# Where the mask of an attention is added: half of its score tiles move from TensorE to VectorE

## The reference

```
x = layernorm(x + L0(x, adj))   # attention of one head, 128 features
x = layernorm(x + L1(x, adj))   # attention of 8 heads of 32 features, the layer of this change
x = layernorm(x + L2(x, adj))   # sums over neighbours
x = layernorm(x + L3(x, adj))   # 4 heads of 256, then one more, then a feed-forward part
```

```
q, k, v = split_heads(h @ W.T + b)
scores  = einsum('bhqd,bhkd->bhqk', q, k) / sqrt(32)
scores  = where(adj == 0, -inf, scores)
attn    = softmax(scores);  out = (attn @ v) @ Wo.T + bo
```

## Time and profile before

| | |
|---|---|
| time, median of 3 runs | 3092.38 us (3091.72 to 3095.64) |
| the profiled execution | 3093.04 us, its span 3091.3 us |
| mean granted TensorE clock | 0.943 of full speed |
| L663, the mask on PE | 512 matmuls of 128 x 512, 134.1 us busy |
| L871, the exp of the scores | 512 instructions, 263.9 us busy |

### The profile page before, as it was taken

How to read it: one execution, slowest core, us unless ns; L and a number is a source line. 1 busy time by engine, 2 the same in 40 slices (tenths; PEclk the granted TensorE clock), 3 DMA queues, 4 the chain that set the end, 5 groups by cost and what they waited for, 6 DMA issues and landing times.

```text
span 3091.3 us, 47649 instructions
## 1 busy us (share of the span) xinstructions
PE 2725.8 (88%) x17668; PEld 2029.7 (66%) x17668; DVE 2070.4 (67%) x5503; ACT 1223.4 (40%) x2273; POOL 824.4 (27%) x640
## 2 busy tenths in 40 slices
PE   0679989899998989989898998989899998989976
PEld 0447776767767676766767677676767767676664
DVE  3547485775848677584867758486775858677563
ACT  0224435353443535344352543435254343524341
POOL 0113231322313232232323222232322323232231
PEclk9889989999898999989899998989999898999987
DMA  4000000000000000000000000000000000000000
GB/s 124 7 14 1 8 14 1 15 8 15 8 8 14 1 15 8 15 8 8 14 1 15 8 15 8 8 14 1 14 8 15 8 8 14 1 8 8 1 8 7
DMA packets 29763, 36.74 MB, mean 12 GB/s; under 512 B 2272, under 2 KB 23648, under 8 KB 29536
## 3 DMA queue, kind: packets, MB, share of 16 engines
q1 hardware_dynamic: 29536, 33.69, 3.7%
HBM read 25.30 MB, written 8.39 MB: 11 GB/s over the span
## 4 chain that ended last, share of the span: by engine, by line
PE 57%; DVE 23%; issue 8%; ACT 6%; POOL 4%; SPq 1%; DMA 1%; DVEq 0%; POOLq 0%; ACTq 0%
PE bank L587 12%; PE bank L546 9%; PE bank L784 7%; DVE bank L1077 5%; PE bank L673 4%; PE bank L561 4%; PE bank L679 4%; PE bank L540 4%; PE bank L663 3%; PE bank L656 3%; POOL exp_b L472 3%; DVE picked L1044 2%; PE bank L793 2%; DVE o_t L1121 2%; PE bank L713 2%
## 5 line engine op out<-in xcount | busy, mean ns | idle before, releaser
L472 POOL TENSOR_TENSOR exp_b<-exp_b,edge_t 128x512 int32<-128x512 int32 x320 | 455.0, 1437 | 1075.9 <-DVE exp_b L1065 1075.9
L587 PE MATMUL bank<-vals_b,exp_b 128*128 128x257 f32 x2560 | 662.6, 404 | 75.4 <-POOL exp_b L472 67.3
L587 PEld LDWEIGHTS bank<-vals_b,exp_b 128*128 128x128 f32 x2560 | 483.4, 198 | 231.8 <-POOL exp_b L472 117.7
L923 ACT ACTIVATE h_sb<-bank,rden_g_b 128x256 f32<-128x256 f32 x320 | 151.6, 474 | 692.5 <-DVE rden_g_b L1221 692.5
L1077 DVE CUSTOM_DVE_ANT_0 bank<-bank,edge_bias 128x512 f32<-128x512 f32 x512 | 338.9, 720 | 22.4 <-PE bank L605 21.5
L1065 DVE TENSOR_TENSOR exp_b<-exp_b,low_b 128x512 f32<-128x512 f32 x320 | 271.6, 870 | 93.1 <-ACT low_b L839 90.8
L1044 DVE CUSTOM_DVE_ANT_0 picked<-bank,edge_bias 128x512 bf16<-128x512 f32 x384 | 241.5, 683 | 108.9 <-PE bank L561 108.9
L871 ACT ACTIVATE exp_a<-bank 128x512 f32<-128x512 f32 x512 | 263.9, 608 | 89.4 <-PE bank L663 89.4
L818 ACT ACTIVATE vals_b<-bank 128x512 f32<-128x512 f32 (+1 forms) x192 | 100.9, 536 | 485.5 <-PE bank L784 280.7
L460 POOL TENSOR_TENSOR rstd_a<-var_eps_a,neg_half 128x4 f32<-128x4 f32 x48 | 51.2, 1067 | 777.5 <-DVE var_eps_a L1021 777.5
L784 PE MATMUL bank<-wo_sb,ht_all 128*128 128x259 f32 x1024 | 233.6, 383 | 0.8 <-ACT ht_all L818 0.8
(11 more groups left out here) (185 smaller groups left out, 5409.5 us busy)
## 6 DMA issues: line engine op xcount, KB each, us to landing
x_t<-in_x_t SPq DMA_DIRECT2D x16, 512.0 KB, 3.6
xa<-in_x SPq DMA_DIRECT2D x16, 512.0 KB, 3.7
out<-h_sb SPq DMA_DIRECT2D x16, 512.0 KB, 2.9
exp_b<-in_adj SPq DMA_DIRECT2D x1, 1024.0 KB, 7.1
edge_t<-in_adj_t SPq DMA_DIRECT2D x1, 1024.0 KB, 9.2
wo_sb<-in_L_gnn_W_out SPq DMA_DIRECT2D x1, 1024.0 KB, 11.7
ht_all<-in_L_gnn_a_heads SPq DMA_DIRECT2D x4, 256.0 KB, 8.6
exp_a<-in_L_gnn_W_heads SPq DMA_DIRECT2D x2, 512.0 KB, 4.3
```

Source lines behind the costliest of these rows:

```text
L472: pool.tensor_tensor(high_exp(idx, j).bitcast(I32), high_exp(idx, j).bitcast(I32), edge_t[:, j, :], ALU.mult)\
L587: last = pe.matmul(bank(key)[:, i * width:(i + 1) * width], high_exp(idx, c)[:, t * P:(t + 1) * P], vals[:, c, 0:width], start=c == 0, sto ...
```

## The change

For group 1 the four L663 matmuls of a tile are gone; the L660 product is the last, and raises the bank's signal. In each `st 1 t` phase DVE now adds `edge_bias_t` to the bank and writes the sum to `exp_a` (four instructions of 128 x 512 a tile, 16 a batch), and it is DVE that sets the bank free. ACT takes the exponential in place in `exp_a`, after DVE. `pv` waits for ACT as before. The wait for room in `exp_a` moves from ACT to DVE. Group 0 stays.

```diff
+ADDED = (0,)
+        def place_free(g, t):
+            at = g * T + t - 2
+            return [product_of("a01") if at < 0 else sig.value("weighed", (at // T, at % T)) if at % T < T - 1 else
+                    product_of(("sum", at // T))]
                     for hh in heads:
-                        pe.matmul(bank(key)[:], first_row_r[at, :], max_rows[at, g, :], start=False, stop=False)
-                    for hh in heads:
+                        shifted = pe.matmul(bank(key)[:], first_row_r[at, :], max_rows[at, g, :], start=False,
+                                            stop=g not in ADDED)
+                        if g not in ADDED:
+                            shifted.then_inc(filled(key), 1)
+                    for hh in heads if g in ADDED else ():
                         pe.matmul(bank(key)[:], ident_b[:], edge_bias_t[:, t, :], start=False, stop=True)\
...
-                        pe.wait_ge(*after(b, moved(("st", g, t, hh))))
+                        pe.wait_ge(*after(b, moved(("st", g, t, hh)) if g in ADDED else sig.value("exp_1", (t, hh))))
...
+                        else:
+                            act.wait_ge(*after(b, moved(key)))
+                            act.activation(exp1(g, t, hh), exp1(g, t, hh), ACT.Exp, scale=SCALE1)\
+                               .then_inc(sig.raised("exp_1", (t, hh)), 1)
...
-                for g in range(G1):
-                    yield "on", g
-                    weighted(g)
+                yield "on", 0
+                weighted(0)
+                for t in range(T):
+                    yield "st", 1, t, 0
+                    for hh in range(HG):
+                        key = ("st", 1, t, hh)
+                        for count in highest(b, product_of(key), *([] if hh else place_free(1, t))):
+                            dve.wait_ge(*count)
+                        dve.tensor_tensor(exp1(1, t, hh), bank(key)[:], edge_bias_t[:, t, :], ALU.add).then_inc(emptied(key), 1)
+                yield "on", 1
+                weighted(1)
```

More of the change, by code:

```diff
@@ L866, in exps1 @@
                     for hh in heads_of("st", p):
[L867 to L871, removed]
+                        key = ("st", g, t, hh)
+                        if g in ADDED:
+                            for count in highest(b, product_of(key), *([] if hh else place_free(g, t))):
+                                act.wait_ge(*count)
+                            act.activation(exp1(g, t, hh), bank(key)[:], ACT.Exp, scale=SCALE1).then_inc(emptied(key), 1)
+                        else:
+                            act.wait_ge(*after(b, moved(key)))
+                            act.activation(exp1(g, t, hh), exp1(g, t, hh), ACT.Exp, scale=SCALE1)\
+                               .then_inc(sig.raised("exp_1", (t, hh)), 1)
                 yield "q", 0
```

## The result

The changed kernel took 3148.03 us (median of 4 runs, 3146.33 to 3149.13) against 3092.55 us on the same chip: ratio 1.0177, 95% interval 1.0159 to 1.0195. The forecast was 3145 us. Its profiled execution has a span of 3145.8 us and a mean granted clock of 0.931 (before: 3091.3 us, 0.943).

A forecast was written before the change was run, and what follows sets the result against it. PE's order was taken as the limit of the stretch; 2.2 us of waits net of removed matmuls plus 1.3 us of clock, over 15 passes, gave 52.5 us on 3093.04, forecast 3145 us, range 3110 to 3175 us.

The forecast's parts named there:

- the waits: New PE waits less removed matmuls, up to `val 0`: 2.2 us a pass; alone, as a rival, 3125 us, chance 0.28.
- the clock: Half clock for 3 us after PE's long wait before `st 1 2`, in most passes: 1.3 us a pass.
- The first wait: Before `st 1 1`: PE idles 2.0 us until DVE's adds clear the banks, starting 1.15 us later than before.
- The second: At `ht 2 0`: `a3 2 3`'s three steps stand behind the adds and end at 1057.9; PE is 1.15 us late.
- The third: Before `st 1 2`: bank 7's copy comes behind ACT's exponentials; PE idles 2.7 us and starts 3.7 us late.
- The fourth: At `a3 3 0`: POOL's product ends at 1065.7, so `pv 1 1` starts 3.05 us late.
- hold up nothing: Between `pv 1 1` and `val 0`: DVE's last four adds lie beside other PE work and delay nothing.
- The sum: Waits and clock together: 3.5 us a pass over 15 passes, 52.5 us; forecast case, chance 0.50.
- The pass that runs alone: The one pass where `mid` runs alone: between -3.5 us and +2.5 us, taken as 0.
- The removed matmuls: Group 1's four L663 matmuls a tile: 0.87 us a tile, 3.5 us a pass, paying in full unless something comes later.
- faster: Rival: the adds find room before PE asks, so all 3.5 us a pass stay; 3040 us, chance 0.06.

The follow-up runs named there:

- held: The changed kernel with useless PE work added: `a3 2 3` done twice, the transposes of `ht 2 0` three times; 3144.90 us, ratio 1.0164.
- copy_held: `held` with ACT also taking the copy out of bank 7 before the exponentials of `st 1 1`; 3133.36 us, ratio 1.0127.
- no_mask: The kernel before with the mask of group 1 left out on every engine; 3070.35 us, ratio 0.9927.
- four_tiles: The kernel before with DVE adding the mask in tiles 2 and 3 of both groups; 3040.62 us, ratio 0.9831.
- tile0: The kernel before with DVE adding the mask in tile 0 of group 1 only; 3117.43 us, ratio 1.0077.
- late_tiles: The kernel before with DVE adding the mask in tiles 2 and 3 of group 1 only; 3074.25 us, ratio 0.9932.

## Why the prediction was right

The sign and the size came out, 3148 against 3145 us, and so did the path: adds behind other work, banks cleared late, PE waiting. That the size is so near is in part luck: of the two terms of the sum the waits were 0.8 us a pass too small and the clock 0.7 us too large, and the two errors cancel.

- *The first wait (banks of `st 1 1`)*: 1055.5 forecast, 5.03 us after `st 1 0` measured, which is 1055.55. Right.
- *The second (`a3 2 3` behind the adds)*: its three steps ended 7.34 us into the pass, as forecast (1057.9). But `pv 1 0` started at 9.09 instead of 7.5 us: the walk listed the banks of every score tile and not that of `pv`'s sums, bank 0, which DVE's add now clears. A missed wait of 1.1 us or more, hidden behind the third as long as the clock is full.
- *The third (bank 7 behind ACT's exponentials)*: real, as `held` and `copy_held` show, but in the change the half-clocked `pv 1 0` is later than it.
- *The fourth (POOL's product)*: `copy_held` shows it next in line.
- *From `pv 1 1` to `val 0`*: "hold up nothing" failed. From `st 1 3` to `val 0` took 6.57 us, where 6.83 less 0.87 and 0.1 of wait give 6.1. `pv 1 3` keeps pace with the last adds: L684 takes 1.40 us instead of 1.06. With what small delays come before, the term without the clock was 29.68 - 26.70 = 3.0 us a pass and not 2.2.
- *The clock*: 1.3 us a pass forecast, 0.6 measured. The step that failed is its place: I had it fall after the third wait and hit `st 1 2` and `a3 3 0`, but it fell after the first or about the second and hit `pv 1 0`. Of the 1.7 us that this product took longer, 1.1 lie in time that was waited anyway. In the pass at 1068.97, where it fell earliest, `val 0` came at 29.68 us, as in `held`: nothing lost.
- *The sum*: 3.5 forecast, 3.6 measured in the stretch (30.3 - 26.7); from `st 1 0` to `st 1 0` a pass went from 180.9 to 184.4 us on the mean.
- *The pass that runs alone*: taken as 0, was 2.9 us (from `st 1 0` of the first pass to that of the next, 153.2 before, 156.1 after), just beyond the bound of 2.5.
- *The removed matmuls* "pay in full": refuted by `no_mask`. The walk itself had the waits right, so the number did not suffer, but in this order the rival "faster" at 3040 us was out of reach: with no mask at all in group 1 the kernel takes 3070 us. That an order with other turns would not reach it is not shown. The 3040 us that `four_tiles` reached needed group 0.

## What to carry to other kernels

Before moving work from the busiest engine, ask what that engine runs into when the work is gone, and try it with the work simply left out: here the first two of four masks returned 0.1 us. When engines share a written order, an added instruction costs by its place, not by its length: the same four 0.68 us adds cost 1.9 us in one tile and gained in another. List for every bank not only the next product of the same kind but the next user of any kind. And read a small effect where the edit is, not from the total: a clock that fell or held some 60 us behind the edit moved the totals by as much as some of the effects.

## What the runs showed of the hardware

Useless PE work in a wait can pay for itself: `held` adds some 3 us of it a pass and its stretch is 0.6 us shorter, since the granted clock stays at 1.00, 2.4 GHz, through waits of up to 1.06 us. In the pass of the change shown above, where PE had been busy for 1.10 us of 3, it went to 0.50, 1.2 GHz. The same wait need not lower it each time: behind the first wait of 1.90 us it fell in 5 of 15 passes of `tile0`, and the L0 products behind a wait of 1.40 us ran at half clock in 13 of 14 passes before and in none of `late_tiles`. What half clock costs depends on when it comes: 3.57 us instead of 1.85 for `pv 1 0` cost 0.6 us of a pass, since the banks were not clear either.
